# Cross-attention kernel: score maxima over a full 128-row contraction with zeroed shift rows, and the maxima turned on VectorE instead of TensorE

## The reference, cut to what matters

```python
qn = layer_norm(q, q_norm_g, q_norm_b)
kvn = layer_norm(kv, kv_norm_g, kv_norm_b)
Q = (qn @ Wq)...;  K = (kvn @ Wk)...;  V = (kvn @ Wv)...      # 16 heads of 32
scores = einsum('bhqd,bhkd->bhqk', Q, K) / sqrt(32)
attn = softmax(scores, axis=-1)
ctx = einsum('bhqk,bhkd->bhqd', attn, V)
out = q + gelu(ctx @ Wo + bo)                                  # exact gelu
```

## Time and profile before

| | |
|---|---|
| median of 3 runs | 3264.93 us (3263.69 to 3266.2) |
| the profiled execution | 3262.8 us, span 3261.0 us |
| TensorE, VectorE, ScalarE, GpSimd busy | 99%, 69%, 70%, 71% of the span |
| chain that ended last | TensorE 97% |
| granted TensorE clock | 0.998 of full |
| DMA queue of SyncE | 339.03 MB in 186000 packets, 60.0% of 16 engines |

### The profile page before, as it was taken

One profiled execution on the slowest core, in us unless ns is written; L12 is line 12 of the kernel. 1 busy time (PEld: TensorE's weight loads), 2 busy tenths in 40 slices (PEclk: granted clock), 3 DMA queues, 4 the chain that ended last, 5 costly groups with the idle time before them and its releaser, 6 DMA issues.

```text
span 3261.0 us, 49855 instructions
## 1 busy us (share of the span) xinstructions
PE 3230.8 (99%) x16611; PEld 2135.1 (65%) x16611; DVE 2256.9 (69%) x4769; ACT 2280.3 (70%) x3985; POOL 2313.9 (71%) x1544
## 2 busy tenths in 40 slices
PE   8999999999999999999999999999999999999998
PEld 5566666666666666666666666666666666666664
DVE  6667667676676676666766766766667767667664
ACT  5677666777767777667767667776777676677765
POOL 3676776777677767777776677777767776777765
PEclk9999999999999999999999999999999999999999
DMA  5655656566556656565665566665656655666653
GB/s 142 87 108 107 108 104 116 91 111 107 107 104 104 111 107 107 104 118 89 111 109 106 105 102 111 109 104 104 120 86 112 107 107 107 100 111 108 105 79 76
DMA packets 186721, 343.02 MB, mean 105 GB/s; under 512 B 20561, under 2 KB 20577, under 8 KB 186466
## 3 DMA queue, kind: packets, MB, share of 16 engines
q1 hardware_dynamic: 186000, 339.03, 60.0%
q10 hardware_dynamic: 466, 0.80, 0.2%
HBM read 104.87 MB, written 33.55 MB: 42 GB/s over the span
## 4 chain that ended last, share of the span: by engine, by line
PE 97%; DVE 1%; ACT 1%; issue 1%; DMA 0%; POOL 0%; SPq 0%; ACTq 0%; POOLq 0%; DVEq 0%
PE gen L856 43%; PE score L883 16%; PE score L876 15%; PE ctx L903 14%; PE gen L847 4%; PE gen L943 4%; PE gen L965 1%; DVE maxes L706 1%; DMA k_stack<-k_nat 0%; ACT q_stack L617 0%; PE score L788 0%; ACT probs L563 0%; DVE stats L725 0%; PE gen L837 0%; POOL probs L475 0%
## 5 line engine op out<-in xcount | busy, mean ns | idle before, releaser
L475 POOL TENSOR_TENSOR probs<-probs 128x1024 f32<-128x1024 f32 x762 | 1800.3, 2392 | 287.8 <-PE ctx L903 281.6
L706 DVE TENSOR_REDUCE maxes<-score 128x1 f32<-128x512 f32 x2048 | 1294.9, 680 | 217.5 <-PE score L883 213.9
L563 ACT ACTIVATE probs<-score 128x512 f32<-128x512 f32 x2048 | 1090.2, 621 | 141.1 <-PE score L876 137.5
L883 PE MATMUL score<-k_stack,q_stack 96*128 96x512 f32 x2048 | 761.2, 413 | 3.3 <-DVE maxes L706 1.8
L876 PE MATMUL score<-q_stack,k_stack 128*128 128x512 f32 x2048 | 696.4, 406 | 6.6 <-ACT q_stack L617 6.5
L883 PEld LDWEIGHTS score<-k_stack,q_stack 96*128 96x128 f32 x2048 | 378.2, 188 | 221.3 <-ACT probs L563 83.6
L876 PEld LDWEIGHTS score<-q_stack,k_stack 128*128 128x128 f32 x2048 | 374.7, 188 | 199.9 <-DVE maxes L706 64.4
L903 PE MATMUL ctx<-probs,v_sb 128*32 128x512 f32 x4096 | 492.5, 598 | 0.0
L856 PE MATMUL gen<-cT,w_k 128*128 128x512 f32 x1536 | 461.7, 400 | 0.2 <-DVE q_nat L688 0.2
L856 PE MATMUL gen<-w_v,cT 128*128 128x512 f32 x1536 | 461.4, 395 | 0.0
L856 PE MATMUL gen<-xT,w_q 128*128 128x512 f32 x1536 | 447.9, 394 | 0.0
(11 more groups left out here) (89 smaller groups left out, 2765.4 us busy)
## 6 DMA issues: line engine op xcount, KB each, us to landing
k_stack<-k_nat SPq DMA_DIRECT2D x384, 256.0 KB, 7.6
q_stack<-q_nat SPq DMA_DIRECT2D x381, 256.0 KB, 5.6
tok<-in_x SPq DMA_DIRECT2D x132, 256.0 KB, 11.0
tok<-in_ctx SPq DMA_DIRECT2D x128, 256.0 KB, 12.0
res<-in_x SPq DMA_DIRECT2D x124, 256.0 KB, 2.7
out<-res SPq DMA_DIRECT2D x124, 256.0 KB, 2.1
probs<-in_L_xattn_Wq SPq DMA_DIRECT2D x1, 1024.0 KB, 8.2
probs<-in_L_xattn_Wk SPq DMA_DIRECT2D x1, 1024.0 KB, 10.4
```

Source lines behind the costliest of these rows:

```text
L475: pool.tensor_tensor(probs[:, c + 1, heads], probs[:, c + 1, heads], probs[:, c, heads], ALU.add).then_inc(pool_added, 1)
L563: act.activation(probs[:, n, part, :], score_at(s, "st", i)[:], ACT.Exp, scale=SCALE).then_inc(exp_done, 1)
L706: dve.tensor_reduce(maxes[:, u1 % 2, SROW + i:SROW + i + 1], score_at(s, "s", i)[:], AX_X, ALU.max, negate=True).then_inc(max_done, 1)
L883: pe.matmul(score_bank(pe, b, s, "s", i)[:, :], q_stack[0:KROWS, u1 % 2, n, P * part:P * (part + 1)], k_stack[0:KROWS, u1 % 2, n, :], star ...
```

## The change

What it does, part by part:

- `s` contracts over all 128 rows instead of 96. For that, rows 96 to 127 of the slot of `q_stack` must be zero when `s` runs: a new tensor `zero_rows` in DRAM (256 KB) is filled once from a zeroed tile (`act_out`) by SyncE's `prepare`, and each `rq` in SyncE's loop first waits for `stack_used`, issues a DMA of `zero_rows` to those 32 partitions, and only then waits for `free["q"]` and issues its three DMAs. The first `s` of a step waits for `rows_cleared` as well.
- The maxima no longer pass through TensorE and PSUM. `md` on VectorE now writes the high part of the 16 columns (rounded on writing to the split format), the low part by one fused multiply and subtract, and turns the 128x32 result by four 32x32 transposes into rows 96 to 127 of `max_hl`. The items `m`, `mh` and `ml` are gone, and with them `m`'s turn of the three `GEN` banks.
- The lists of all engines are new.
- Copying `bias_all` out of PSUM at the start moves a few lines, and two small constants go.

```diff
     "pe": (
-        "q*3 v q*2 v q v st*2 v*2 s st v s st s v*2 st s st s z v st*3 s v*2 st*2 s st k v s*4 pv st s st*2 o s "
-        "st s k s*2 pv m k o*2 k o k*2",
-        "o st*2 o st*3 q st q*4 st q st*3 z x k*3 x st*2 x st k*2 s k st s st*2 pv s x s x s x s pv s x s*2 o*3 "
-        "s*2 x o s o*2 s o s o*2 s o s o*3 m",
-        "o*4 s o s k s k s st k s st z st s st s q st q st s st*2 k st*3 k s st k st*4 pv s*2 q s q s*2 q s*2 q "
-        "pv m",
-        "k q k v q v k*2 st*3 k st*2 q st*2 k q st q st q st*2 z st*4 v st v s*3 pv s*2 v s*2 v s*2 v s v s*2 v*2 "
-        "s*2 v s*2 v pv m",
+        "q*3 v q v*2 q*2 st*3 s v*2 s st v*2 st v s st v st s v st s*2 st z st v st v st s k s*3 pv st s st k "
+        "s*2 o st*2 s o s*2 pv o k o k*3 o",
+        "st*3 o st*2 q*2 st*2 q st q*3 st*2 x z k*4 st k st x st s st*2 k s*2 st x pv s*3 x s x pv x s*3 x "
+        "o*2 s o*4 s*4 o s o*2",
+        "o*2 x o*3 s*2 o*3 s o s k s st k s z st k st*2 s k st*2 q st s st q st*2 k st s st k st*4 pv s*2 q s "
+        "q*2 s*2 q s*2 pv",
+        "k*6 q*2 st*3 q*2 st*2 v st*2 v st q st q st*3 z st*3 v*2 s*3 st pv s*3 v*2 s*2 v s v s v s*2 v s v "
+        "s*2 v s pv",
     ),
     "act": (
...
-        "st*6 k st*5 q st*4 split st v*2 mh mx*4",
+        "k st*16 q split v*2 mx*4",
     ),
     "dve": (
...
-        "k zt zr zb cn q s*16 md ml",
+        "k zt zr zb cn s*3 q s*13 md",
     ),
     "sp": (
         "load*8 rq rk store res",
-        "rq rk store res store",
-        "store first_res rk rq first_res",
+        "rq rk store",
+        "res store first_res rk rq store first_res",
         "rq rk",
...
+                    sp.wait_ge(act_out_free, 1)
+                    sp.dma_start(zero_rows.rearrange("r (c n) -> (r c) n", n=D), act_out[:]).then_inc(zeros_stored, 16)
...
+                        if kind == "rq" and valid(b2):
+                            if known(b) and (b, s) == (-1, 2):
+                                sp.wait_ge(zeros_stored, 16)
+                            wait(sp, stack_used, NU * b2 + u2 + 1)
+                            sp.dma_start(raw(q_stack[SROW:P, u2 % 2, :, :]),
+                                         zero_rows.rearrange("r (c n) -> r c n", n=D)).then_inc(rows_cleared[u2 % 2], 16)
                         if kind in ("rq", "rk") and valid(b2) and not (kind == "rq" and known(b) and (b, s) == (-1, 2)):
                             which = kind[1]
                             wait(sp, free[which], NU * b2 + u2 + 1)
-                            wait(sp, stack_used, NU * b2 + u2 + 1)
                             if which == "q":
                                 restack(sp, u2, q_nat, q_stack, ((0, 0), (1, 0), (2, 1)), q_stacked)
                             else:
+                                wait(sp, stack_used, NU * b2 + u2 + 1)
                                 restack(sp, u2, k_nat, k_stack, ((0, 0), (1, 1), (2, 0)), k_stacked)
...
                         if kind == "md" and valid(b1):
                             wait(dve, max_done, 16 * (t1 + 1))
+                            dve.tensor_reduce(max_split[:, 0:SHIFTS // 2], maxes[:].unsqueeze(2), AX_X,
+                                              ALU.max).then_inc(max_high, 1)
+                            wait(dve, max_high, t1 + 1)
+                            dve.scalar_tensor_tensor(out=max_split[:, SHIFTS // 2:SHIFTS], in0=maxes[:], scalar=ones[:, 0:1],
+                                                     in1=raw(max_split[:, 0:SHIFTS // 2]), op0=ALU.mult,
+                                                     op1=ALU.subtract).then_inc(max_low, 1)
                             wait(dve, shift_rows, NC * t1)
+                            wait(dve, max_low, t1 + 1)
+                            for g in range(P // SHIFTS):
+                                rows = slice(SHIFTS * g, SHIFTS * (g + 1))
+                                dve.transpose(max_hl[SROW:P, rows], raw(max_split[rows, :])).then_inc(max_turned, 1)
...
                             if i == 0:
                                 wait(pe, q_stacked, 48 * (t1 + 1))
+                                wait(pe, rows_cleared[u1 % 2], 16 * (NU // 2 * b1 + u1 // 2 + 1))
                                 wait(pe, k_stacked, 48 * (t1 + 1))
-                            pe.matmul(score_bank(pe, b, s, "s", i)[:, :], q_stack[0:KROWS, u1 % 2, n, P * part:P * (part + 1)],
-                                      k_stack[0:KROWS, u1 % 2, n, :], start=True, stop=True).then_inc(s_full, 1)
+                            pe.matmul(score_bank(pe, b, s, "s", i)[:, :], q_stack[:, u1 % 2, n, P * part:P * (part + 1)],
+                                      k_stack[:, u1 % 2, n, :], start=True, stop=True).then_inc(s_full, 1)
```

More of the change, by code:

```diff
@@ L166 @@
             GEN.append((_kind, {"v": _s // (NU - 1), "o": -1, "x": 1}[_kind], _n, 2 * NC if _kind == "x" else NC))
-        if _part == 0 and _kind in ("q", "k", "m", "z"):
-            _off = _s + {"q": 2, "k": 2, "m": 1, "z": -1}[_kind]
+        if _part == 0 and _kind in ("q", "k", "z"):
+            _off = _s + {"q": 2, "k": 2, "z": -1}[_kind]
             GEN_AT[(_kind, _off % NU)] = len(GEN)
@@ L180, in build @@
     B = x.shape[0]
+    zero_rows = nc.dram_tensor("zero_rows", (SHIFTS, HU * D), F32).ap()
     with ExitStack() as es:
@@ L232, in build @@
         gen = [ps(f"gen{i}") for i in range(NGEN)]
-        full = {k: sem(f"{k}_in_psum") for k in "vomzxqk"}
-        free = {k: sem(f"{k}_out_of_psum") for k in "vomzxqk"}
+        full = {k: sem(f"{k}_in_psum") for k in "vozxqk"}
+        free = {k: sem(f"{k}_out_of_psum") for k in "vozxqk"}
         st_full = sem("st_full")
@@ L243, in build @@
         x_hi = sem("x_hi")
-        max_cut_done = sem("max_cut_done")
-        max_copied = sem("max_copied")
+        max_high = sem("max_high")
+        max_low = sem("max_low")
+        max_turned = sem("max_turned")
         shift_rows = sem("shift_rows")
@@ L248, in build @@
         stack_used = sem("stack_used")
+        zeros_stored = sem("zeros_stored")
+        rows_cleared = [sem(f"rows_cleared{i}") for i in range(2)]
         q_stacked = sem("q_stacked")
@@ L609, in batch @@
                                            bias=bias_k[:, u2:u2 + 1]).then_inc(k_hi, 1)
-                        if kind == "mh" and valid(b1):
-                            wait(act, full["m"], NU * b1 + u1 + 1)
-                            wait(act, free["m"], NU * b1 + u1)
-                            act.activation(max_cut[SROW:P, :], gen_at("m", u1)[SROW:P, 0:P], ACT.Identity,
-                                           scale=cut_sign[SROW:P, 0:1]).then_inc(max_cut_done, 1)
                         if kind == "mx" and valid(b1):
-                            wait(act, free["m"], NU * b1 + u1 + 1)
+                            wait(act, max_turned, HU * (NU * b1 + u1 + 1))
                             act.activation(q_stack[SROW:P, u1 % 2, :, P * n:P * (n + 1)],
-                                           raw(max_hl[SROW:P, :]).unsqueeze(1).to_broadcast([SHIFTS, HU, P]),
+                                           max_hl[SROW:P, :].unsqueeze(1).to_broadcast([SHIFTS, HU, P]),
                                            ACT.Identity, scale=chunk_mask[SROW:P, n:n + 1]).then_inc(shift_rows, 1)
@@ L697, in batch @@
                     t1, t2, tp = NU * b1 + u1, NU * b2 + u2, NU * bp + up
+                    if known(b) and (b, s) == (0, 0):
+                        dve.wait_ge(bo_mm, 1)
+                        dve.tensor_copy(bias_all[:], ctx_ps[:]).then_inc(bo_ready, 1)
+                        dve.wait_ge(bo_ready, 1)
                     for kind, n, part in PLAN["dve"][s]:
@@ L702, in batch @@
                             i = NC * n + part
-                            if i == 0:
-                                wait(dve, full["m"], t1 - 1)
                             wait(dve, s_full, 16 * t1 + i + 1)
-                            dve.tensor_reduce(maxes[:, u1 % 2, SROW + i:SROW + i + 1], score_at(s, "s", i)[:], AX_X, ALU.max,
+                            dve.tensor_reduce(maxes[:, i:i + 1], score_at(s, "s", i)[:], AX_X, ALU.max,
                                               negate=True).then_inc(max_done, 1)
@@ L961, in batch @@
                                 mm.then_inc(full[kind], 1)
-                        if kind == "m" and valid(b1):
-                            bank = gen_bank(pe, b, "m", u1)
-                            wait(pe, max_copied, t1 + 1)
-                            pe.matmul(bank[:, 0:P],
-                                      maxes[:, u1 % 2, :], ident[:], start=True, stop=True,
-                                      is_transpose=True).then_inc(full["m"], 1)
             all_batches(pe, batch)
```

43 lines of the change are left out of this document (10 added, 33 removed), and 12 rows, old and new, of the table ORDER.

## The result

The changed kernel takes 3461.55 us (median of 4 runs, 3460.17 to 3463.0), against 3264.31 us for the kernel before on the same chip (4 runs). The ratio is 1.0603, with a 95% interval of 1.0585 to 1.0622: 197 us slower. The forecast was 3320 us, with a range from 3238 to 3398. The direction was right, the size was not. The profiled execution took 3462.57 us, its span is 3460.8 us.

A forecast was written before the change was run, and what follows sets the result against it. TensorE, busy 99% of the span, was taken to bound the kernel. Zeroing stalls +84, `m` -12, 128 rows -7 and bank waits -10 gave +55 us on 3262.8, forecast 3320 us, range 3238 to 3398.

The forecast's parts named there:

- the bound on the maxima: After `md` on VectorE: fused step and four transposes take at most 1.8 us, up to 0.65 us later than before.
- so their sum costs nothing: ScalarE and VectorE: operations removed and added cost no time, as both engines have 30% free.
- the late maxima: Rival: the new fused step and transposes delay the four `mx`; +20 us, 3285 us, chance 0.08.
- The zeroing DMA, +84 us: TensorE stands at the first `s` of steps 0, 1, 2 for 0.89, 0.80, 0.94 us, as q and k land later.
- Z: Drain time of the zeroing DMA in SyncE's queue, delaying all six q and k DMAs: 1.11 us, between 0.64 and 1.92.
- B: Step 0 to 1, `pv` to first `s`: room falls from 1.34 to 0.31 us, TensorE stalls 0.80 us.
- C: Step 1 to 2, `pv` to first `s`: room falls from 1.98 to 0.17 us, TensorE stalls 0.94 us.
- A: Step 3 to 0, `pv` to first `s`: room falls from 0.98 to 0.22 us, TensorE stalls 0.89 us.
- The hidden zeroing: Rival: zeroing doesn't move the last k landing, gains stand alone; 3236 us, chance 0.28.
- The rooms: Slack before TensorE stands at the first `s` of steps 0, 1, 2 in the new lists: 0.22, 0.31, 0.17 us.
- The gains, -29 us: On TensorE: -12 us for `m` removed, -7 us for `s` over 128 rows, -10 us for fewer PSUM bank waits.
- the bank waits: TensorE's waits for PSUM banks in crowded places, about 21 us in all; half taken as saved, -10 us.

The follow-up runs named there:

- `mx` first: Kernel before plus the change without low part or new lists, ScalarE's step 1 `mx` ahead of the second gelu: 3286.62 us; with 96 rows and no zeroing 3287.6 us.
- q earlier: Changed kernel without the low part, with the q copies placed earlier in the step 3 lists of ScalarE and VectorE: 3301.06 us, 1.0115.

## Why the prediction was wrong

**The step that failed** is the bound on the maxima: "The new fused step and four transposes are bounded by five times that 0.36 us, 1.8 us, as each is smaller than that form: up to 0.65 us later". The four transposes kept to it, 0.92 us in all. The fused step alone took 1.65 us on average and 2.27 at most. The row I bounded it by, L771, reads `gen`, which is in PSUM; `maxes` and `max_split` are both in SBUF, where GpSimd's additions (2393 ns each, 762 of them) hold it. L771 itself ran beside these additions 126 times and never took more than 361 ns, so as a row it could not show the hold. I had taken size for the measure of likeness, and it was the memory in which the operands lie; no run moved an operand of the subtraction to PSUM, so this part rests on comparing rows. With that bound, "so their sum costs nothing" and a chance of 0.08 for the late maxima followed. Two runs show it: halved additions (the longest hold falls from 2270 to 1254 ns and 80 us come back) and the low part left out (172 us come back).

That the direction came out right is mostly luck. The forecast was slower because of the zeroing DMA, and 172 of the 197 us came from a step that stood in the sum at nothing.

**The zeroing DMA, +84 us.** This step was wrong too, and in the other direction. I said that the landing moves by Z = 1.11 us. Compared with and without it, it moves by 0.40 and 0.28 us at B and C of the versions without the low part, by 0.38, 0.05 and 0.16 us in the kernel before, by 0.59, 0.46 and 0.18 us in the old lists with `mx` first, and not at all at A of the new lists. The hidden zeroing was the nearest of my cases: but for that one 0.59, Z in effect was under the 0.5 us that I named. The landings at A and B that matched the 16.4 to 16.6 us of the prediction (16.65 and 16.80) matched for other reasons. At A, SyncE's queue shows it:

```profile
1639.46 0.32 SPq L420 DMA_DIRECT2D q_stack<-zero_rows  x1
1640.74 1.85 SPq L355 DMA_DIRECT2D q_stack<-q_nat  x3
1642.69 1.86 SPq L355 DMA_DIRECT2D k_stack<-k_nat  x3
```

The `pv` is at 1638.38. The zeroing is issued 1.08 us later, but the q DMAs stand until 1640.74, although the zeroing needs only 0.32 us of the queue: they wait for the q copies, which the new lists place after `st*16` on ScalarE and after `s*3` on VectorE. The copy on VectorE ends at 1640.72. Moving the copies moved the landing (q earlier, -0.73 us). At B it is the late maxima again: the k copy (L610) stands behind `mx` in ScalarE's list and the k DMAs are issued at 1680.12. Without the low part B is back at 15.66. My prediction never asked whether the copies would still be in time in the new lists.

**The rooms.** Of the counts of items between `pv` and first `s` nothing was seriously off: without the low part the first `s` of steps 0, 1 and 2 waits for about 1.4, 0.24 and 0.39 us, 2.03 us or 65 us in all, against 84 forecast. The sum was near, its parts were not: A is mostly the q copies, and B and C are a third of what I had.

**The gains, -29 us.** In the changed kernel -32 us is left over when the waits and the clock are taken out. Without the low part it is more: 65 us of waits, and a batch longer by only 0.74 us (24 us), so 41 us of gains. These two are differences of sums and not measured item by item; `m` and the bank waits were not separated. Of the 7 us for 128 rows, 6 came in the pace, 3 ns for each of the 2048 `s`. The 7 ns between the two rows that I compared were another thing in part, since `s` and `st` have other neighbours in the lists: with only rows and zeroing changed, the mean duration of an `s` falls from 413 to 411 ns in the kernel before and from 406 to 403 in the new lists. And where the lists had no room for it the time did not follow: 0.9995 and, between the two versions with `mx` first, 1 us. By the rule of the Trainium skill ("TensorE: Matmul & The Clock Gate", the step by step of Part 2): the time of the kernel before with 128 rows (0.9995) agrees with it, the pace is off by 3 ns in the mean and 6 in the median.

**What was not in the prediction at all** is the clock: an estimated 41 us of the loss come from matmuls at a granted clock of 0.50 behind the longest wait. I had counted each wait once, by its own length.

**What stays open.** Why the reduction, the transposes and the operations of one column, from SBUF to SBUF as well, are not held; no run changed their form. Why a further GpSimd addition sometimes goes ahead of a VectorE operation that already waits (2.8 and 4.5 us) and sometimes, behind the same residual addition, does not. And whether a subtraction with one operand in PSUM would make the change pay: by the version without the low part, which is 0.8% slower, it would not.

## What to carry to other kernels

When a change adds a small operation to VectorE beside a busy GpSimd, price it by a row whose operands lie in the same memories, and ask how long GpSimd's instructions are: 16 columns in SBUF cost 235 ns alone and mostly up to the whole 2.39 us of the instruction beside them, in some versions even more. A wide spread between minimum and median in the view by line, where the form is the same, is the sign of such a hold; lay the other engine's ends beside its ends. And in a tightly ordered kernel a wait that is removed by moving an item tends to return at the next item, so count the whole ring of the move.

## What was not expected of the hardware

- A VectorE operation of 128x16 from SBUF to SBUF, with two sources or with one, ended 28 to 38 ns after the running GpSimd addition in 127 of 128 cases, and took 235 (two sources) and 175 ns (one source) when free. A reduction of the same size (170 ns), 32x32 transposes (205 ns), one-source operations of one column (at most 155 ns) and fused operations with one of two inputs in PSUM (at most 361 and 752 ns) beside such additions were never held.
- The hold is not bounded by one GpSimd instruction: 2.8 us in one place of 21 of 32 batches in one version and of 20 in another, and 4.5 us once in a third, beside additions of 2.39 us.
- After TensorE had stood for 2.01 us the granted clock was 0.50 from about 1679.6 to 1683.0, beginning 1 us after it resumed.
- A DMA of 256 KB from DRAM to 32 partitions ahead of six restacks in one queue delayed the last of them by 0.05 to 0.6 us where nothing else held it, although the restacks themselves land 1.92 us apart.
- With the lists unchanged, the gap from the matmul before to an `s` was 233 ns over 96 rows and 227 ns over 128 in the median, and 3 ns apart in the mean.
